# A recommendation tower on one core: the first step's x operands picked by TensorE, the second batch of rows gathered in one go, and GpSimd splitting from unit 4 of round 0

## What is computed

```python
e = jnp.stack([tbl_0[ids[:, 0]], ..., tbl_38[ids[:, 38]]], axis=1)      # [1024, 39, 16]
h = x = e
for i, (W, b) in enumerate(zip(Ws, bs)):                                # three layers, 128 outputs each
    z = jnp.einsum('bfd,bgd->bfgd', x, h)                               # every pair of rows, elementwise
    cur = relu(jnp.einsum('bfgd,fgl->bld', z, Wr) + b[None, :, None])
    if i != 2:
        h = cur[:, :64]; direct = cur[:, 64:]
    else:
        direct = cur
z = concat(directs, axis=1).sum(-1)                                     # [1024, 256]
h = relu(concat([z, dense_ctx]) @ W_top1 + b_top1)
y = relu(h @ W_top2 + b_top2) @ W_top3                                  # [1024, 1]
```

## Time and profile before

| | us |
|---|---|
| median of 3 runs | 1298.85 (1298.71 to 1299.05) |
| the profiled execution | 1300.39 |
| its span | 1298.5 |
| PE busy | 1229.6 (95%) |
| POOL busy | 1068.2 (82%) |
| DVE busy | 1046.4 (81%) |
| ACT busy | 750.6 (58%) |

### The profile page before, as it was taken

The page is one execution under the profiler, slowest core; times in us unless marked ns, Lnnn a source line. Parts: engine busy times, 40 slices in busy tenths (PEclk is TensorE's granted clock), DMA queues, the critical chain, the costliest instruction groups (busy, mean ns, idle before and its releaser), DMA issues.

```text
span 1298.5 us, 13246 instructions
## 1 busy us (share of the span) xinstructions
PE 1229.6 (95%) x4084; PEld 745.5 (57%) x4084; DVE 1046.4 (81%) x943; ACT 750.6 (58%) x931; POOL 1068.2 (82%) x627
## 2 busy tenths in 40 slices
PE   0379999999999999999999999999999999999999
PEld 0335555655665656655665556656656566666655
DVE  2069998888888888988888888888888888988941
ACT  1135665656555666556556656566556677777643
POOL 7528899888988898888989798888888778889942
PEclk9989999999999999999999999999999999999999
DMA  9195566655555666655556676545556665556100
GB/s 184 37 216 121 125 142 145 145 119 110 124 117 116 140 145 145 136 115 111 123 114 129 144 145 135 131 103 125 119 119 141 144 142 108 130 118 161 33 0 1
DMA packets 103424, 157.68 MB, mean 121 GB/s; under 512 B 20954, under 2 KB 33131, under 8 KB 103245
## 3 DMA queue, kind: packets, MB, share of 16 engines
q1 hardware_dynamic: 93179, 154.16, 53.5%
q0 software_dynamic: 10176, 2.70, 2.2%
HBM read 152.91 MB, written 6.19 MB: 123 GB/s over the span
## 4 chain that ended last, share of the span: by engine, by line
PE 87%; POOL 4%; DVE 4%; issue 3%; ACT 1%; DMA 1%; SPq 0%; DVEq 0%; ACTq 0%; POOLq 0%
PE curM L858 36%; PE curM L881 11%; PE curM L873 11%; PE curM L874 11%; PE curY L858 10%; POOL emb L305 3%; DVE z L566 2%; PE xk L847 2%; PE h L964 1%; PE curY L881 1%; PE curY L873 1%; PE curY L874 1%; DVE zl L619 1%; POOL zl L316 1%; ACT h L725 1%
## 5 line engine op out<-in xcount | busy, mean ns | idle before, releaser
L316 POOL TENSOR_TENSOR zl<-z,zh 128x1024 fp32r<-128x1024 f32 (+1 forms) x299 | 724.1, 2433 | 118.1 <-ACT zh L698 112.6
L566 DVE TENSOR_TENSOR z<-xr,h 128x1024 f32<-128x1024 f32 x576 | 677.4, 1216 | 154.5 <-PE curM L858 129.1
L698 ACT ACTIVATE zh<-z 128x1024 fp32r<-128x1024 f32 (+1 forms) x376 | 396.4, 1057 | 387.3 <-DVE z L566 243.4
L858 PE MATMUL curM<-z,wf 128*128 128x512 f32 (+2 forms) x1194 | 537.7, 600 | 0.0
L305 POOL DMA_INDIRECT emb<-in_tbl_dram,idx x312 | 337.6, 1082 | 100.1 <-issue 57.5
L873 PE MATMUL curM<-zh,wl 128*128 128x512 f32 (+1 forms) x642 | 340.7, 531 | 4.2 <-ACT zh L698 4.2
L858 PEld LDWEIGHTS curM<-z,wf 128*128 128x128 f32 (+2 forms) x1194 | 208.5, 188 | 195.2 <-issue 171.6
L874 PE MATMUL curM<-zh,wh 128*128 128x512 f32 (+1 forms) x642 | 251.8, 392 | 0.0
L881 PE MATMUL curM<-zl,wh 128*128 128x512 f32 (+1 forms) x642 | 200.7, 394 | 6.1 <-DVE zl L619 3.6
L873 PEld LDWEIGHTS curM<-zh,wl 128*128 128x128 f32 (+1 forms) x642 | 121.7, 190 | 72.7 <-issue 47.4
L725 ACT ACTIVATE h<-curM,bias 32x512 f32<-32x512 f32 (+1 forms) x198 | 127.9, 646 | 57.5 <-DVE z L566 51.1
(11 more groups left out here) (107 smaller groups left out, 436.9 us busy)
## 6 DMA issues: line engine op xcount, KB each, us to landing
xr<-xT SPq DMA_DIRECT2D x384, 192.0 KB
xs<-xT SPq DMA_DIRECT2D x288, 156.0 KB
xq<-xT SPq DMA_DIRECT2D x64, 256.0 KB
...
```

What stands on the lines that cost most here:

```text
L316: nc.gpsimd.tensor_tensor(zl[0:n, SNUM[r, u] % NL, :], z[0:n, z_slot(r, u), :], zh[0:n, SNUM[r, u] % NH, :], ALU.subtract).then_inc(lo_poo ...
L566: return nc.vector.tensor_tensor(z[:, slot, :].rearrange("p (a n) -> p a n", a=2), x, h, ALU.mult)
L698: nc.scalar.activation(zh[0:n, SNUM[r, u] % NH, :], z[0:n, z_slot(r, u), :], ACT.Copy).then_inc(hi_ready, 1)
L858: mm = nc.tensor.matmul(cur[:, :], wf[rows, full_at(u), a, :], z[rows, z_slot(r, u), a * N:(a + 1) * N], start=start and i == 0, stop=stop ...
```

## The change

The change has three parts, which are built into the start of the program.

- **x of the first step.** Matrices of zeros and ones (`picks`, `picks_xr`) are made by DVE from the identity, in a part of xr[1] that is free then (24 copies). PE multiplies them with xc[0], which gives the seven tiles of xs for step 0 (`pick`) and, in round -3 ahead of unit 21, the first three of the nine column blocks of xr for step 0. They land in the PSUM banks h1, curM[0] and curM[1], and ACT copies them to xs and xr[0] (`copy_picked`, and three copies in round -3). The loads of these from xT go, and DVE waits on `x0_copied` for them. PE's matmuls on the identity stand ahead of the turns now, wait for the first 32 gathered fields and are 40. Steps 0 and 1 are turned before the first picks, step 2 among them. ACT's copy of xc of step 2 stands at the start of round -2. SP loads xs of step 1 first, then the other two thirds of xr and xq of step 0, and then writes step 2.
- **Gathers.** The 39 gathers of the second batch follow the first 39 with no wait on `x_begun`, and none is left in round 0.
- **Splits.** In round 0 POOL subtracts from unit 4 on: units 5, 7, 11 and 13 move from DVE to POOL.

```diff
+POOL_FROM = 4
...
-    return "D" if k == "G" and (r < 0 or (r == 0 and u < 16)) else k
+    return "D" if k == "G" and (r < 0 or (r == 0 and u < POOL_FROM)) else k
...
-EARLY_FIELDS, BETWEEN = 4, 29
...
-WARM = 28
+WARM = 40
+
+PICKED = (1, 3, 4, 5)
...
+        wrapped = xr[1][0:F, 20 * L:20 * L + XR]
+        picks = xr[1][0:F, 21 * L:21 * L + T0 * R0].rearrange("p (t m) -> p t m", m=R0)
+
+        picks_xr = xr[1][0:F, 28 * L:28 * L + 12 * Q].rearrange("p (f m) -> p f m", m=Q)
...
-                if r == 0:
-                    b, gathers = 1, list(range(BETWEEN, F))
...
-            for f in range(BETWEEN):
-                if f == EARLY_FIELDS:
-                    pool.wait_ge(x_begun, 1)
+            for f in range(F):
                 gather(f, 1, gathered[1])
...
@@ -467,26 +473,23 @@
             write_x(0, 0)
             sp.wait_ge(xc_copied, 2)
             write_x(1, 1)
+            sp.wait_ge(xT_written[1], 32)
+            for p in range(4):
+                sp.wait_ge(z_ready, NUM[-3, C_END + p] + 1)
+                load_xs(1, p)
             sp.wait_ge(w_hi, HI_OPS)
             sp.wait_ge(w_lo, LO_OPS)
             sp.wait_ge(w_full, FULL_OPS)
             sp.wait_ge(xT_written[0], 32)
-            for p in range(4):
-                load_xs(0, p)
+            for k in range(1, 3):
+                load_xr(0, 0, k)
+            load_xq(0, 0)
             sp.wait_ge(xc_copied, 3)
             write_x(2, 0)
-            sp.wait_ge(xT_written[1], 32)
-            for p in range(4):
-                sp.wait_ge(z_ready, NUM[-3, C_END + p] + 1)
-                load_xs(1, p)
-            for k in range(3):
-                load_xr(0, 0, k)
-            load_xq(0, 0)
             sp.wait_ge(xT_written[0], 64)
             for p in range(4):
                 sp.wait_ge(z_ready, NUM[-2, C_END + p] + 1)
                 load_xs(2, p)
-            sp.sem_inc(x_begun, 1)
             for k in range(3):
                 load_xr(1, 1, k)
             load_xq(1, 1)
...
+            dve.wait_ge(ident_ready, 1)
+            nc.vector.tensor_copy(wrapped[:, 0:F], ident[0:F, 0:F]).then_inc(picks_ready, 1)
+            nc.vector.tensor_copy(wrapped[:, F:XR], ident[0:F, 0:XR - F]).then_inc(picks_ready, 1)
+            dve.wait_ge(picks_ready, 2)
+            for t in range(T0):
+                for k in range(K):
+                    nc.vector.tensor_copy(picks[:, t, k * F:(k + 1) * F],
+                                          wrapped[:, K * t + k:K * t + k + F]).then_inc(picks_ready, 1)
+            nc.vector.tensor_copy(picks_xr, ident[0:F, 0:12].unsqueeze(2).to_broadcast([F, 12, Q])).then_inc(picks_ready, 1)
             dve.wait_ge(dense_turned, 1)
...
                 if u < NQ:
                     if u % 3 == 0:
-                        dve.wait_ge(xr_loaded[s % 2][u // 3], 64 * (s // 2 + 1) + 32 * LOOP * j)
+                        if (s, u) == (0, 0):
+                            dve.wait_ge(x0_copied, PICKED[3] + 3)
+                        elif s % 2 == 0 and u == 0:
+                            dve.wait_ge(xr_loaded[0][0], 64 * (s // 2) + 32 * LOOP * j)
+                        else:
+                            dve.wait_ge(xr_loaded[s % 2][u // 3], 64 * (s // 2 + 1) + 32 * LOOP * j)
...
-                dve.wait_ge(xs_loaded[p], each * (s + 1) + each * LOOP * j)
+                if s == 0:
+                    dve.wait_ge(x0_copied, PICKED[p])
+                else:
+                    dve.wait_ge(xs_loaded[p], each * s + each * LOOP * j)
...
                 if r == -2:
+                    copy_xc(2, 0)
+                    act.wait_ge(x0_copied, PICKED[3] + 3)
                     for i in range(7):
                         take0(r, i, j)
                 for u in range(UNITS):
                     if present(r, u):
                         hi(r, u, j)
+                    if (r, u) == (FIRST, UNITS - 1):
+                        for q in range(3):
+                            act.wait_ge(picked, 4 + q + 1)
+                            bank = (curM[1][:, :], h1[:, 0:N], h1[:, N:2 * N])[q]
+                            nc.scalar.activation(xr[0][:, q * N:(q + 1) * N], bank, ACT.Copy).then_inc(x0_copied, 1)
...
+            def copy_picked(p, bank, a, nt, n):
+                act.wait_ge(picked, p + 1)
+                nc.scalar.activation(xs[0:n, (2 * p + a) * N:(2 * p + a + nt) * N], bank[0:n, 0:nt * N],
+                                     ACT.Copy).then_inc(x0_copied, 1)
+
             copy_first_emb()
-            for t in range(3):
-                copy_xc(t, 0)
+            copy_xc(0, 0)
+            copy_xc(1, 0)
+            act.wait_ge(w_lo, LO_OPS)
+            act.wait_ge(w_full, FULL_OPS)
+            copy_picked(0, h1, 0, 2, R0)
+            copy_picked(1, curM[0], 0, 1, R0)
+            copy_picked(1, curM[1], 1, 1, R0)
+            copy_picked(2, h1, 0, 2, R0)
+            copy_picked(3, curM[0], 0, 1, R0_LAST)
             act.wait_ge(small_loaded, 16 * 6)
...
+                        if (r, u) == (FIRST, C_END + 1):
+                            pe.wait_ge(x0_copied, PICKED[2])
+                            for q in range(3):
+                                bank = (curM[1][:, :], h1[:, 0:N], h1[:, N:2 * N])[q]
+                                nc.tensor.matmul(bank, picks_xr[:, 4 * q:4 * q + 4, :].rearrange("p f m -> p (f m)"),
+                                                 xc[0][:, :], start=True, stop=True).then_inc(picked, 1)
+                        if u == C_END and r == -2:
+                            pe.wait_ge(x0_copied, PICKED[3] + 1)
                         if u == C_END and r >= -1:
...
-            pe.wait_ge(emb_copied, 1)
-            for t in range(3):
-                turn(t, 0, 0)
-
+
+            pe.wait_ge(gathered_first, 16 * FIRST_FIELDS)
             for c in range(WARM):
                 nc.tensor.matmul(h1[:, c % DQ * P:(c % DQ + 1) * P], ident[:, :], ident[:, :], start=True, stop=True)
+
+            def pick(t, bank):
+                n = rows0(t)
+                return nc.tensor.matmul(bank[0:n, :], picks[:, t, 0:n], xc[0][:, :], start=True, stop=True)
+
+            pe.wait_ge(emb_copied, 1)
+            turn(0, 0, 0)
+            turn(1, 0, 0)
+            pe.wait_ge(picks_ready, 3 + T0 * K)
             pe.wait_ge(dense_copied, 2)
+            pe.wait_ge(xc_copied, 1)
+            pick(0, h1[:, 0:N])
+            pick(1, h1[:, N:2 * N]).then_inc(picked, 1)
+            pick(2, curM[0])
+            pick(3, curM[1]).then_inc(picked, 1)
+            turn(2, 0, 0)
+            pe.wait_ge(x0_copied, 1)
+            pick(4, h1[:, 0:N])
+            pick(5, h1[:, N:2 * N]).then_inc(picked, 1)
+            pe.wait_ge(x0_copied, 2)
+            pick(6, curM[0]).then_inc(picked, 1)
             pe.wait_ge(w_hi, HI_OPS)
             pe.wait_ge(w_lo, LO_OPS)
             pe.wait_ge(w_full, FULL_OPS)
```

4 lines of the change are left out of this document (3 added, 1 removed).

## The result

| | before | after |
|---|---|---|
| median | 1298.78 us (1297.95 to 1299.05, 4 runs) | 1359.74 us (1357.57 to 1363.14, 4 runs) |
| ratio, 95% interval | | 1.0473 (1.045 to 1.0495) |
| profiled execution | 1300.39 us, span 1298.5 | 1360.24 us, span 1358.4 |

A forecast was written before the change was run, and what follows sets the result against it. PE was taken to bound the kernel from 157.00 on, so only an earlier round 1 counts: start 4.4 plus round 0 4.1 is 8.5 us, 1298.85 - 8.5 = 1290.3 us, range 1287.0 to 1294.8.

The forecast's parts named there:

- Gathers … I charge nothing; the cover is 1.5 us at least: Second batch's 39 gathers end between 101.4 and 117.4, early enough for POOL's first subtraction in round 0; cost zero.
- item 1: Start: 80 identity passes from 45.1 take 11.1 us plus half a pause, 0.5, ending at 56.7; bounds 54.6 and 58.3.
- Items 1 to 3 of the start: Identity matmuls end at 56.7, DVE's copies add 0.3, the turn starts at 57.0, xc is there at 58.5.
- Item 2: Start: DVE's 24 small copies at about 33 us cost nothing there; 0.3 us added for possibly delayed gathers.
- Item 4: Start, from xc to round -3's end: 30 PE passes at 0.43, plus 0.70 and 1.38, make 15.0 us.
- my slower rival: PE runs the picks at the low clock: 15.0 us become 30, 6.5 slower, 1305.4 us; chance 0.05.
- If PE's clock is at half in the picks: Sign that the prediction is wrong; it expected clock 1.00 from the first product to round -3's end at 73.5.
- Round 0: Four subtractions leave DVE and ten gathers leave POOL, so round 0 gives 4.1 us; bounds 5.07 and 3.1.
- Distances behind the start: Order from ACT's copies to round -1 stays unchanged and DVE runs without pause, so the start's 4.4 us is handed on.
- the next load is late instead: Rival: later loads hold DVE at its old 85.64, leaving only round 0's 4.1 us; 1294.8 us, chance 0.08.
- POOL's subtraction lands on the path: Rival: PE waits for each of four moved subtractions in round 0, 4.7 us eating the 4.1; 1295.0 us, chance 0.06.
- the start's bounds: The start's gain of 4.4 us was bounded by 6.5 and 2.2, with the 0.3 for gathers left out or doubled.

The follow-up runs named there:

- run 3: Kernel before with only the second batch's 39 gathers sent in one go, without the wait on x_begun: 1343.72 us, ratio 1.0345.
- run 2: Changed kernel with the second batch's gathers as before, four and then a wait on x_begun, ten in round 0: 1320.27 us, ratio 1.0165.
- run 16: Changed kernel with 200 waits that are already met at the head of PE's queue: 1303.39 us (1298.23 to 1304.86, 4 runs), ratio 1.0059.
- run 17: Changed kernel with 100 waits that are already met at the head of PE's queue: 1301.95 us, ratio 1.0037.
- run 15: Kernel before, splits from unit 4, gathers 4 to 38 released at the first product, plus 26 already met waits on SP's queue: 1293.88 us, ratio 0.9982.
- run 13: Kernel before, splits from unit 4, ten gathers released at the first product and 25 at x_begun, none in round 0: 1299.56 us, ratio 1.0019.
- run 8: Kernel before with 24 dependent subtractions on POOL behind the four early gathers, ahead of its wait: 1300.9 us, ratio 1.0035.
- run 14: Kernel before with splits from unit 4 and all 35 later gathers released at x_begun: 1310.92 us, ratio 1.0108.
- run 1: Changed kernel with 28 matmuls on the identity in place of 40: 1359.82 us, ratio 1.0469.
- run 11: Changed kernel with 16 matmuls on the identity in place of 40: 1358.54 us, ratio 1.0461.
- run 5: Changed kernel with no matmuls on the identity, gathers in one go: 1302.4 us, ratio 1.005.
- run 10: Changed kernel, gathers held until the third picked copy, nine long identity matmuls, picks replaced by 128 rows of other data: 1319.82 us, ratio 1.0163.
- run 9: Changed kernel, gathers held until the third picked copy, nine long identity matmuls, real picks of 39 rows: 1325.88 us, ratio 1.021.
- run 6: Changed kernel without identity matmuls, second batch's gathers held until three picked tiles are copied: 1303.79 us, ratio 1.0043.
- run 7: Changed kernel, gathers held until three picked tiles are copied, six identity matmuls of 512 columns ahead of the turn: 1301.87 us, ratio 1.003.
- run 4: Kernel before with only POOL's splits from unit 4 of round 0, its ten gathers left there: 1303.83 us, ratio 1.0038.

## Why the prediction was wrong, and where it was right

**"Gathers … I charge nothing; the cover is 1.5 us at least" is the step that failed.** I asked when the gathers end (the last ran from 100.28 to 101.2, at the early bound of 101.4, and POOL never held round 0), and what else POOL had to do. I never asked what a row of gathers does to the other engines. Two conditions are shown to act together. One is the gathers: PE's queue kept as it was and only the gathers changed, the pause goes from about 1 to 52 us (run 3); held back, it ends early (run 2). Run 3's edit also takes the wait and the signal of `x_begun` out of the queues, so run 2, where the stall ends with the gathers, is the stronger of the two. The other is what stands in the queues: the gathers kept and only met waits added, the stall is gone (runs 16, 17, and 15 on SP).

The clue was in the earlier trace rows: the pause of 1.03 with "issue" as releaser in the middle of identical matmuls, for which I put 0.5 us into item 1 as if it belonged to the matmuls. I take it, without a run that shows it, for the short form of this stall, since SP crawls beside it, in a part of the trace of before that I hadn't used: its issues come one per 1.40 us from 33 us on, and the first load from xT is issued at 61.74, 4.2 us behind the last write ahead of it, where run 13, with the same queue of SP, needs 0.6. From 60 to 62 the DMA engines are 0.24 busy in before and 0.81 in run 13. SP's rows, before and then run 13:

```profile
33.04 0.70 SPq L461 DMA_DIRECT2D bt<-in_b_top_dram  x1
34.44 0.70 SPq L462 DMA_DIRECT2D bt<-in_b_top_dram  x1
35.84 0.71 SPq L463 DMA_DIRECT2D wt<-in_W_top_dram  x1
...
61.74 3.96 SPq L391 DMA_DIRECT2D xs<-xT  x11
```
```profile
58.33 4.51 SPq L391 DMA_DIRECT2D xs<-xT  x11
```

So the kernel before seems to pay for the stall as well. In runs 8, 13, 14 and 15, where SP doesn't crawl here, the first product comes 6.9 to 7.0 us behind xc, not 8.71, and the seven copies start at 73.6 to 77.2, not 78.07, all with x of step 0 from HBM. Part of what the picks were to save was this.

That the missing thing is the delivery of instructions to the engines is argued, not shown. For it speak "issue" as releaser, one pace for PE, DVE and SP whatever the instruction, and that added instructions move it. What in the queues decides it stays open: a position in one queue (the 98th or 99th of PE in the changed kernel and runs 1 and 11) fails for 100 waits, and run 5, with the identity matmuls gone, passes it at 76.6 us beside gathers without a pause. The Trainium skill, Runtime: NRT & Kernel Launch, Instruction fetch mechanics, says that an engine's instructions are refilled in blocks of 16 KiB and that crossing a boundary is "mostly hidden". If the stall is such a crossing, that rule would have it next to nothing, and the trace of after has 58 us of it.

**Items 1 to 3 of the start.** Run 16 tells what they were worth without the stall; its trace is of the fastest of its four executions. The identity matmuls end at 56.9 (56.7 was forecast; 80 passes in 11.48 us, 11.1 + 0.5), the turn starts at 56.72 (57.0), the first product at 61.67 (61.5), against 64.75 before. In run 17 the turn starts at 55.29 and the first product at 60.25. They were right within their bounds, with some luck in item 1: there is no pause for its 0.5 us, and the matmuls took that much longer. Item 2, DVE's copies at no cost, held on the path even while they crawled.

**Item 4, "30 x 0.43", was mis-sized, and this is my slower rival.** Counted from the end of ACT's xc, 15.2 us were worked out; the changed kernel takes 24.7, run 16 21.5 and run 17 26.4. The count of passes and 0.43 at full clock are right (the first four picks: eight passes in 3.7 us), but in the later ones a pass takes 0.85 (two in 1.91, four in 3.62); PE's clock is granted at 0.50 for 17.1 us from 122.1. "Against it: from 45.1 on PE now has work with gaps under 1 us" was the mistake. In run 16 PE isn't idle from 45.40 until 81, and the windows show its clock fall twice behind 39-row picks:

```profile
58.00:63.90 5.90, 5.90 (x17) 2.96 (x17) 1.86 (x2) 3.00 (x5) 4.68 (x5) 1.00 0.25 49
63.90:70.70 6.80, 6.80 (x9) 2.00 (x7) 3.19 (x4) 2.56 (x3) 4.97 (x7) 0.50 0.74 189
70.70:74.10 3.40, 3.40 (x8) 1.32 (x8) 3.40 (x4) 1.36 (x3) 2.60 (x3) 1.00 0.60 155
74.10:77.50 3.40, 3.40 (x8) 2.33 (x8) 0.43 (x1) 0.90 (x2) 2.67 (x3) 0.50 0.94 242
```

The first rise, at 70.7, stands behind unit 20's passes of 117 rows. After a like fall, run 10 with 128 rows was back at full clock at 62.0, run 9 with 39 only at 86.2. I took a 39-row pass for one of 117 or 128. The Trainium skill, TensorE: Matmul & The Clock Gate, What's actually happening, calls the throttled state the default that activity releases; I took a fed PE for activity, and the trace shows that feeding it with 39 rows is not enough. So the first part of the change, x of step 0 from PE, doesn't pay here: runs 5, 6, 7, 16 and 17 have it without the big stall, and all are 0.3 to 0.6% slower than before. "If PE's clock is at half in the picks" is one of the prediction's own signs of being wrong.

**Round 0** gave 3.84 us (forecast 4.1, bounds 3.1 and 5.07). Right: the cause, four subtractions moved off DVE and no gathers, holds, since run 4 with the gathers left loses instead. **Distances behind the start**, unchanged to 0.01 us, were right too, also in run 16, where the start is near the forecast time (7.57 and 29.45). So the rivals "the next load is late instead" and "POOL's subtraction lands on the path" fall.

**Slips in the prediction's sums.** With item 1's ends of 54.6 and 58.3 and the 0.3, the start's bounds are 6.8 and 2.5 and not 6.5 and 2.2. And if the xr picks or unit 20 went, 3.2 - 1.7 = 1.5 or 3.2 - 2.6 = 0.6 us would show, not 2.2 to 1.9. The forecast uses neither.

**The sum again, with what was measured:** +61.25 - 0.25 + 2.71 - 3.84 = +59.87. In run 16's profiled execution, without the stall: copies +1.7, round 0 -3.8, so -2.1, its span 1296.4 against 1298.5. Its other executions took longer (median 1303.39), and no trace shows why.
